# A two-layer graph network on one core: the stretch behind the softmax reordered by halves of the nodes

## The chip, the core and the metric

The kernel runs on one core of a Trainium2 chip. A core has TensorE (PE, matmuls; its weight loads have rows of their own, PEld), VectorE (DVE), ScalarE (ACT), GpSimd (POOL) and SyncE (SP, which only starts transfers here), and 16 DMA engines that all queues share. The metric is the device time of one execution in microseconds, lower is better.

## The reference

There are 256 nodes with 1024 features. Layer 0 sends messages over 8192 edges and ends in an update of the nodes, layer 1 is a graph attention without softmax. Both end in a residual sum and a layer norm over the features:

```python
# layer 0: alpha is a softmax per target over the edges' logits
z_f = segment_sum(alpha[:, None] * n_f[edge_src], edge_dst, N)
nf2 = concatenate([n_f, z_f], axis=1)                 # 256 x 2048
h_new = relu(nf2[:64] @ W_hn + b_hn)                  # nodes 0 to 63
o_new = relu(nf2[64:] @ W_on + b_on)                  # nodes 64 to 255
x1 = layernorm(x + concatenate([h_new, o_new]))
# layer 1
h = x1 @ W                                            # 256 x 1024
al, ar = h @ a_l, h @ a_r
e = exp(-leaky_relu(al[src] + ar[dst], 0.1))
h_prime = segment_sum(e[:, None] * h[dst], src, N) / (segment_sum(e, src, N)[:, None] + 1e-5)
out = layernorm(x1 + elu(h_prime))
```

## The kernel before

Half 0 is nodes 0 to 127 and half 1 is nodes 128 to 255; a tile holds one half on its 128 partitions. Every weight matrix is streamed in chunks of 128 rows x 1024 columns, two to a transfer, in the order of the list `stream`; chunk numbers n count along it. SP starts each transfer of two chunks into one of 4 places of `W_raw`, once the low parts of the two chunks that lay there are made. For each chunk ScalarE casts `W_raw` to fp32r (`W_hi`, line 432), and VectorE (`W_lo`, line 669) or GpSimd (line 364) subtracts that from the original; `by_pool(n)` gives every fourth chunk (n % 4 == 3) behind chunk 55 to GpSimd. The two parts stand in a ring of NB = 4 places, and a place is free once TensorE has counted the chunk four earlier as used (`chunk_used`). A product in full precision is then three products: high by high, high by low, low by high.

Each engine runs its own program in the order in which it is written, and the stages named in `PE_STAGES`, `ACT_STAGES` and `DVE_STAGES` are counts that the others wait for. `link` makes VectorE wait for its own last instruction.

**The update** (chunks 48 to 79, `update`, lines 1261 to 1283) takes `W_hn` and `W_on` alternately, two chunks of each. A chunk of `W_hn` costs 4 matmuls of 512 columns, which give nodes 0 to 63 (line 1273). A chunk of `W_on` costs 4 such for nodes 64 to 127 (line 1273) and 6 more for half 1 (line 1281). Each group of 4 puts the two parts of 64 nodes side by side on the 128 output partitions, so the two halves of partitions have to be added afterwards. The order within a chunk of `W_on` is half 0 first, half 1 behind it, chunk by chunk, up to chunk 79.

**Layer norm of layer 0** (lines 604 to 622 on ScalarE, 952 to 998 on VectorE): ScalarE copies the partitions to be added out of PSUM (stages q0_low, q1_low); VectorE adds the biases from `bn_bc`, the two parts, then relu and the residual; `bn_stats` and `bn_aggr` give mean and variance (line 957, 958), ScalarE the root (line 594), and the normalised half 0 is written by ScalarE (line 611), half 1 by VectorE (line 969). TensorE transposes each half (line 1317, stages x1T0, x1T1), ScalarE and VectorE make the high and low part of the transposed features.

**h** (chunks 80 to 87, `block_by_block`, line 1089): for each group of 4 chunks half 0, then half 1; 6 matmuls a chunk and half, 96 in all. The first matmul comes after both halves have been transposed. Behind the last, VectorE multiplies h by `a_l` and `a_r` with sums (line 1006), TensorE spreads the source scores over all partitions (line 1326), the exponentials times edge counts are made for all 256 x 256 pairs in `PT`, then TensorE makes the row sums (line 1331, 8 rows) and `h_prime` (line 1336, 16 rows: 4 products of 512 columns for each half, each in two rows).

**The end**: for each half ScalarE writes exp and relu of `h_prime` over the row sum (line 635), VectorE makes elu plus residual (lines 1032, 1034), the statistics and the second layer norm; SP starts one transfer of 512 KB for each half of the output (lines 316, 318). GpSimd subtracts one from `x1` for the elu (line 413) behind its last `W_lo`.

Of the kernel before, what the change touches and what calls it, by code (L numbers as in the profile page):

```python
# [16 lines left out]
Q = 64  # L17
# [22 lines left out]
def gnn_two_layers(nc, x, src, dst, W_hh, b_hh, W_oo, b_oo, W_ho, b_ho, W_a, b_a, W_hn, b_hn, W_on, b_on,  # L40
# [6 lines left out]
    with ctx:  # L47
# [36 lines left out]
        small = sb("small", [P, 64])  # L84

# [143 lines left out]
        for k in range(0, 2 * KC, 2):  # L229
            stream += [("hn", W_hn, k), ("on", W_on, k)]  # L230
# [3 lines left out]
        END = {"ooA": 8, "ooB": 16, "hoA": 30, "hh": 40, "hoB": 48, "updx": 64, "upd": 80, "h1": 88}  # L234
# [27 lines left out]
        def lo_count(n, pool):  # L262
# [27 lines left out]
        def _(sp):  # L290
# [24 lines left out]
            sp.wait_ge(act_step, act_at("out0"))  # L315
            sp.dma_start(out[0:P, :], y2[:, 0, :]).then_inc(out_in, 16)
            sp.wait_ge(dve_step, dve_at("out1"))
            sp.dma_start(out[P:N, :], y2[:, 1, :]).then_inc(out_in, 16)
            sp.wait_ge(out_in, 32)
# [3 lines left out]
        def _(pool):  # L323
# [86 lines left out]

            lows(END["hoB"] + NB, len(chunks))
# [5 lines left out]
        def _(act):  # L417
# [150 lines left out]
            act.dma_start(bn_bc[0:Q, 0, :], b_hn.partition_broadcast(Q)).then_inc(biases_in, 16)  # L568
            act.dma_start(bn_bc[Q:P, 0, :], b_on.partition_broadcast(Q)).then_inc(biases_in, 16)
            act.dma_start(bn_bc[:, 1, :], b_on.partition_broadcast(P)).then_inc(biases_in, 16)  # L570
# [5 lines left out]
            highs(END["hoB"], END["hoB"] + NB)  # L576
            act.wait_ge(dve_step, dve_at("maxima"))
# [13 lines left out]
            highs(UX + 4, END["upd"] - 2)  # L591
            def deviation(h):

                sa.activation(deviations[:, h:h + 1], small[:, 41 + 2 * h:42 + 2 * h], ACT.Sqrt, bias=eps_ln[:, 0:1]) \
                    .then_inc(act_step, 1)
# [11 lines left out]
            highs(END["upd"] - 2, END["upd"])  # L607

            def normalise_first_half(dest):

                sa.activation(dest, y1[:, 0, :], ACT.Identity, bias=small[:, 10:11], scale=small[:, 8:9]) \
                    .then_inc(act_step, 1)

            act.wait_ge(dve_step, dve_at("var0"))
            deviation(0)
            act.wait_ge(dve_step, dve_at("scale0"))
            normalise_first_half(x1[:, 0, :])
            act.wait_ge(dve_step, dve_at("var1"))
            deviation(1)
            for h in range(2):  # L620
                act.wait_ge(pe_step, pe_at(f"x1T{h}"))
                sa.copy(xT_hi[:, :, h * P:(h + 1) * P], G0[:, h * D:(h + 1) * D].rearrange("p (c n) -> p c n", n=P)) \
                    .then_inc(act_step, 1)
# [5 lines left out]
            act.wait_ge(dve_step, dve_at("lr"))  # L629
            sa.activation(PT[:], PT[:], ACT.Exp, scale=-1.0).then_inc(act_step, 1)  # L630
            act.wait_ge(dve_step, dve_at("row_sums"))
            for h in range(2):
                act.wait_ge(pe_step, pe_at(f"hp{h}"))
                for part, func in ((y2, ACT.Exp), (y1, ACT.Relu)):
                    sa.activation(part[:, h, :], G1[:, h * D:(h + 1) * D], func, scale=small[:, 6 + h:7 + h]) \
                        .then_inc(act_step, 1)
            warm_up(ACT.Sqrt, 0)
            act.wait_ge(dve_step, dve_at("var2"))
            deviation(0)
            act.wait_ge(dve_step, dve_at("scale2"))  # L640
            normalise_first_half(y2[:, 0, :])
            act.wait_ge(dve_step, dve_at("var3"))
            deviation(1)
# [3 lines left out]
        def _(dve):  # L647
# [289 lines left out]
            lows(UX, UX + NB)  # L937
            for s in range(2):
# [11 lines left out]
            lows(UX + NB + 4, END["upd"] + NB - 2)  # L950

            def statistics(h):

                for g in range(2):
                    link(v.bn_stats(small[:, 16 + 12 * h + 6 * g:22 + 12 * h + 6 * g], y1[:, h, g * 512:(g + 1) * 512]))  # L957
# [403 lines left out]
```

## Time and profile before

| | us |
|---|---|
| median of 3 runs | 383.04 |
| lowest and highest of them | 382.99 to 384.62 |
| profiled execution, its own time | 383.35 |
| its span, first to last instruction | 381.3 |
| TensorE busy, share of the span | 326.5, 86% |
| VectorE busy | 301.9, 79% |
| ScalarE busy | 189.9, 50% |
| GpSimd busy | 136.8, 36% |
| mean granted TensorE clock | 0.934 of 2.4 GHz |

The profiled execution's own time is its span plus 2.05 us. The span can be read in stages by the line numbers of the chain: up to 260 us the first part of layer 0, 260 to 311 us the update, 311 to 328 us the layer norm, 328 to 351 us h, and 351 us to the end scores, `h_prime` and output. Only what lies behind about 230 us is touched by the change.

### The profile page before, as it was taken

Reading aid. Unit: us, or ns where it says so; the run is one execution under the profiler, and the core shown is the slowest. Engines: PE = TensorE matmul, PEld = TensorE weight load, DVE = VectorE, ACT = ScalarE, POOL = GpSimd, SP = SyncE. Lnnn points to the kernel's source line nnn. Section 1 sums busy time; section 2 is a strip of 40 time slices with the busy share of each in tenths; the row PEclk is TensorE's granted clock in tenths of the full one; section 3 lists DMA queues with packets and bytes.
Section 4 is the critical chain, followed back from the end, with each engine's and each line's share of the span. In section 5 each row is a group of like instructions: output and inputs, shape, how many; then the busy total and the mean of one; then the engine's idle time right before and its main releaser. Section 6 shows DMA issues by size and latency. Waiting matters only on the chain.

```text
span 381.3 us, 4671 instructions
## 1 busy us (share of the span) xinstructions
PE 326.5 (86%) x1434; PEld 252.7 (66%) x1434; DVE 301.9 (79%) x400; ACT 189.9 (50%) x289; POOL 136.8 (36%) x202
## 2 busy tenths in 40 slices
PE   2899999999999998999999999638899962898570
PEld 1678877776547866888888887426688841686320
DVE  0799999959799687999999997985677789436445
ACT  3745594220333349788787764250566581251143
POOL 3200070370008002988988773910024231016000
PEclk9999999999999999999999999885999995699685
DMA  7997698899989960002003003333638960000002
GB/s 232 412 400 292 238 345 298 278 244 275 354 297 377 388 243 2 0 3 112 0 2 111 3 3 89 131 110 119 211 106 332 306 250 2 0 2 1 0 0 110
DMA packets 17639, 63.63 MB, mean 167 GB/s; under 512 B 2234, under 2 KB 2236, under 8 KB 17360
## 3 DMA queue, kind: packets, MB, share of 16 engines
q1 hardware_dynamic: 13520, 50.34, 36.2%
q0 software_dynamic: 2096, 8.74, 7.8%
q10 hardware_dynamic: 2000, 4.26, 3.2%
q8 instruction: 13, 0.21, 0.2%
q14 instruction: 10, 0.08, 0.1%
HBM read 60.16 MB, written 3.16 MB: 166 GB/s over the span
## 4 chain that ended last, share of the span: by engine, by line
PE 64%; DVE 25%; DMA 4%; ACT 4%; issue 2%; SPq 0%; DVEq 0%; ACTq 0%
PE ps L1240 20%; PE ps L1067 10%; PE ps L1131 7%; DVE W_lo L669 6%; PE ps L1089 6%; PE ps L1247 3%; PE ps L1273 3%; PE ps L1106 3%; PE ps L1304 3%; PE ps L1336 3%; DMA W_raw<-in_L_gnn_W_dram 2%; PE ps L1281 2%; DMA x_nat<-in_x_dram 2%; DVE tile_val L690 1%; DVE small L957 1%
## 5 line engine op out<-in xcount | busy, mean ns | idle before, releaser
L432 ACT CAST W_hi<-W_raw 128x1024 fp32r<-128x1024 f32 x72 | 73.2, 1046 | 67.9 <-DMA W_raw<-in_L_gnn_W_ho_dram 24.6
L669 DVE TENSOR_TENSOR W_lo<-W_raw,W_hi 128x1024 fp32r<-128x1024 f32 x56 | 73.7, 1342 | 23.2 <-ACT W_hi L432 20.7
L905 DVE SCALAR_TENSOR_TENSOR ps<-ps,wa_bc 128x1024 f32<-128x1024 f32 x74 | 87.6, 1277 | 1.9 <-PE ps L1240 1.9
L364 POOL TENSOR_TENSOR W_lo<-W_raw,W_hi 128x1024 fp32r<-128x1024 f32 x16 | 39.4, 2468 | 82.0 <-ACT W_hi L432 82.0
L1240 PE MATMUL ps<-A_tab,oh 128*128 x148 | 53.5, 443 | 2.2 <-ACT oh L541 2.2
L390 POOL TENSOR_SCALAR sc_r<-irow,keys 128x64 f32<-128x64 f32 x74 | 35.0, 472 | 39.1 <-PE ps L1247 38.7
L1067 PE MATMUL ps<-W_hi,xT_hi 128*128 128x512 f32 x112 | 46.5, 415 | 0.9 <-DVE W_lo L669 0.9
L1240 PE MATMUL ps<-B_tab,oh 128*128 x148 | 46.4, 394 | 0.0
L1067 PE MATMUL ps<-W_lo,xT_hi 128*128 128x512 f32 x112 | 44.1, 394 | 0.0
L547 ACT ACTIVATE sc_l<-sc_l,keys 128x64 f32<-128x64 f32 x74 | 24.6, 341 | 21.8 <-DVE ps L905 15.5
L1067 PE MATMUL ps<-W_hi,xT_lo 128*128 128x512 f32 x112 | 34.5, 390 | 0.0
L391 POOL TENSOR_SCALAR sc_l<-irow,keys 128x64 f32<-128x64 f32 x74 | 33.0, 446 | 0.0
L1247 PEld LDWEIGHTS ps<-sc_r,sc_l 128*128 128x128 f32 x148 | 27.4, 189 | 6.3
L1240 PEld LDWEIGHTS ps<-B_tab,oh 128*128 128x128 f32 x148 | 27.8, 188 | 4.9
L1131 PE MATMUL ps<-W_raw,hh_x 128*128 128x512 f32 x64 | 28.2, 594 | 0.0
L1240 PEld LDWEIGHTS ps<-A_tab,oh 128*128 128x128 f32 x148 | 24.1, 187 | 4.0 <-issue 3.5
L1067 PEld LDWEIGHTS ps<-W_hi,xT_hi 128*128 128x128 f32 x112 | 21.3, 190 | 7.3 <-DVE W_lo L669 2.5
L534 ACT ACTIVATE oh_dist<-key_rows,pcol 128x512 bf16<-128x512 uint8 x37 | 26.1, 707 | 0.0
L1067 PEld LDWEIGHTS ps<-W_lo,xT_hi 128*128 128x128 f32 x112 | 21.4, 191 | 4.7 <-issue 0.7
L1067 PEld LDWEIGHTS ps<-W_hi,xT_lo 128*128 128x128 f32 x112 | 21.2, 189 | 4.6
L1247 PE MATMUL ps<-sc_r,sc_l 128*128 128x64 f32 x148 | 24.0, 247 | 0.0
L541 ACT ACTIVATE oh<-oh_dist 128x512 fp32r<-128x512 bf16 x37 | 23.1, 625 | 0.9 <-PE ps L1240 0.6
(229 smaller groups left out, 546.7 us busy)
## 6 DMA issues: line engine op xcount, KB each, us to landing
W_raw<-in_L_gnn_W_oo_dram SPq DMA_DIRECT2D x8, 1024.0 KB, 9.7
W_raw<-in_L_gnn_W_ho_dram SPq DMA_DIRECT2D x8, 1024.0 KB, 4.9
W_raw<-in_L_gnn_W_hh_dram SPq DMA_DIRECT2D x8, 1024.0 KB, 8.4
W_raw<-in_L_gnn_W_hn_dram SPq DMA_DIRECT2D x8, 1024.0 KB, 5.3
W_raw<-in_L_gnn_W_on_dram SPq DMA_DIRECT2D x8, 1024.0 KB, 6.0
W_raw<-in_L_gnn_W_dram SPq DMA_DIRECT2D x4, 1024.0 KB, 7.6
key_rows<-key_rows_scratch POOLq DMA_DIRECT2D x1, 2304.0 KB, 14.0
table_scratch<-tabs ACTq DMA_DIRECT2D x2, 1024.0 KB, 6.4
```

The costliest lines, as they stand in the source:

```text
L364: ga.tensor_tensor(W_lo[:, ring(n), :], W_raw[:, n // 2 % NS, n % 2, :], W_hi[:, ring(n), :].bitcast(F32), ALU.subtract).then_inc(lo_pool, 1)
L390: ga.tensor_scalar(sc_r[:, t % U, :], irow[:, 1:Q + 1], keys[:, t, 0:1], None, ALU.is_equal)
L391: ga.tensor_scalar(sc_l[:, t % U, 1, :], irow[:, 1:Q + 1], keys[:, t, 1:2], None, ALU.is_equal) \
L432: sa.copy(W_hi[:, ring(n), :], W_raw[:, n // 2 % NS, n % 2, :]).then_inc(hi_made, 1)
L534: sa.activation(oh_dist[:, j % 2, :, :], key_rows[:, :, 2 * j * P:2 * (j + 1) * P], ACT.Abs, bias=pcol[:, 1:2]).then_inc(dist_made, 1)
L547: sa.activation(sc_l[:, t % U, 0, :], sc_l[:, t % U, 1, :], ACT.Copy, scale=keys[:, t, 2:3]) \
L669: v.tensor_tensor(W_lo[:, ring(n), :], W_raw[:, n // 2 % NS, n % 2, :], W_hi[:, ring(n), :].bitcast(F32), ALU.subtract).then_inc(lo_made, 1)
L905: v.scalar_tensor_tensor(acc, acc, 0.0, wa_bc[:], ALU.max, ALU.mult, accum_out=keys[:, t, 2:3]).then_inc(reduced, 1)
L1067: ins = mm(acc[:, m * D + f:m * D + f + 512], x_part(n - first, m), W[:, f:f + 512], start=(n == first and x_part is hi and W is W1), stop ...
L1131: ins = mm(G0[:, f:f + 512], hh_x[:, row // KC, row % KC, :], W_raw[:, n // 2 % NS, n % 2, f:f + 512], start=(row == 0), stop=(row == 2 * ...
L1240: ins = mm(acc[:, n * 512:(n + 1) * 512], oh[:, t // 2 % 2, k, t % 2 * P:(t % 2 + 1) * P], tab[:].rearrange("p q d -> p (q d)")[:, n * 512 ...
L1247: ins = mm(G0[:, bass.ds(column.with_bounds(min_val=0, max_val=15 * Q), Q)], sc_l[:, t % U, :, :].rearrange("p r n -> p (r n)"), sc_r[:, t ...
```

## The change

1. **Order of the update.** The stream takes `W_hn` ahead of `W_on`, so that chunks 76 to 79 are the last four of `W_on` and `W_hn` is through at chunk 75. For chunks 76 to 79 the matmuls of half 0 (`parts` 0) are issued for all four chunks, and the 24 of half 1 behind them. `chunk_used` counts these chunks with the matmuls of half 1. ScalarE then copies q0_low, q1_low between its casts.
2. **Biases by matmul.** The two bias rows come to 64 partitions only, are split into a high and a low part on ScalarE (stage parts) and VectorE, and six matmuls of 512 columns with a pattern `pick` of ones (made by GpSimd) add them into PSUM at the beginning of the update. The additions from `bn_bc` go.
3. **Layer norms.** The sums come with the instruction that adds the residual (`accum_out`); `bn_stats` goes. ScalarE squares the half less its mean, with a sum (`Square`, `deviation`), then takes the root (`root`). Both halves are normalised by VectorE. Residual and partitions of half 0 are merged in two instructions for each 64 nodes (`merge`).
4. **Half 0 leads.** TensorE transposes half 0, starts the first two chunks of h for half 0, and only then transposes half 1. The low parts of chunks 83 and 87 move from GpSimd to VectorE; GpSimd subtracts one from `x1` right behind the transposes.
5. **h and scores.** The last four chunks are multiplied for half 0 (stage h_0), then columns 0 to 511 of half 1 (h_1), then columns 512 to 1023. The scores of half 1 are made in two parts of 512 columns and added. `PT` goes through leaky relu, exp and edge counts by halves.
6. **h_prime and the end.** `h_prime` of half 0 comes ahead of the row sums, half 1 behind them in two parts of 512 columns. Relu is taken before the division and scaled by VectorE. The root's table of ScalarE is no longer called up ahead of the second layer norm. The second output half is normalised half by VectorE and half by ScalarE, and its two parts are started by SP and by ScalarE's queue.

```diff
+        update_order = [("hn", 0), ("on", 0), ("hn", 2), ("on", 2), ("hn", 4), ("on", 4), ("hn", 6), ("hn", 8), ("on", 6),
+                        ("hn", 10), ("on", 8), ("hn", 12), ("on", 10), ("hn", 14), ("on", 12), ("on", 14)]
...
-            return n % 4 == 3
+            return n % 4 == 3 and n < END["upd"]
...
+            pool.wait_ge(gathered, NT)
+            link(ga.memset(pick_f[:], 0.0))
+            for r in (0, Q // 2):
+                link(ga.memset(pick_f[r:r + 1, 0:P], 1.0))
+            ga.nop().then_inc(pick_made, 1)
             lows(END["hoB"] + NB, len(chunks))
...
+            act.wait_ge(pick_made, 1)
+            sa.copy(pick[:], pick_f[:])
+            act.wait_ge(biases_in, 112)
+            sa.copy(bn_parts[:], bn_rows).then_inc(act_step, 1)
             act.wait_ge(dve_step, dve_at("maxima"))
...
+            def deviation(h, waste):
+                sa.activation(waste, y1[:, h, :], ACT.Square, bias=less_mean[:, h:h + 1], accum_out=squares[:, h:h + 1]) \
+                    .then_inc(squared, 1)
+            def root(h, nth):
+                act.wait_ge(squared, nth)
+                sa.activation(deviations[:, h:h + 1], squares[:, h:h + 1], ACT.Sqrt, bias=eps_ln[:, 0:1], scale=1.0 / D) \
...
+            highs(END["hn"], END["hn"] + 2)
+            act.wait_ge(dve_step, dve_at("mean0"))
+            deviation(0, x1[:, 0, :])
+            root(0, 1)
+            highs(END["hn"] + 2, END["upd"])
+            x1_high(0)
+            act.wait_ge(dve_step, dve_at("mean1"))
+            deviation(1, x1[:, 1, :])
+            root(1, 2)
+            x1_high(1)
...
+            link(v.tensor_tensor(bn_parts[Q // 2:Q], bn_rows[Q // 2:Q], bn_parts[Q // 2:Q].bitcast(F32), ALU.subtract))
+            stage("parts")
...
+            dve.wait_ge(act_step, act_at("q0_low"))
+            merge(G0[0:Q, D:2 * D], y2[0:Q, 0, :], slice(0, Q))
+            dve.wait_ge(act_step, act_at("q1_low"))
+            merge(G1[Q:P, 0:D], y2[Q:P, 0, :], slice(Q, P))
+            mean(0, "mean0")
+            low(END["upd"])
+            inverse(0, "sd0")
+            normalise(x1[:, 0, :], y1[:, 0, :], 0)
+            stage("x1_0")
+            dve.wait_ge(chunk_used, END["upd"])
+            link(v.scalar_tensor_tensor(y1[:, 1, :], G1[:, D:2 * D], 0.0, x_nat[:, 1, :], ALU.max, ALU.add,
+                                        accum_out=y_sums[:, 1:2]))
+            mean(1, "mean1")
+            low(END["upd"] + 1)
+            x1_low(0)
+            inverse(1, "sd1")
+            normalise(x1[:, 1, :], y1[:, 1, :], 1)
...
+            for h in range(2):
+                dve.wait_ge(act_step, act_at(f"exp{h}"))
+                link(v.tensor_tensor(PT[:, h, :], PT[:, h, :], S_cnt[:, 0, h, :], ALU.mult))
+                stage(f"ET{h}")
...
+            update(70, END["hn"])
+            update(END["hn"], END["upd"], (0,))
+            update(END["hn"], END["upd"], (1,))
...
+            transpose_x1(0)
+            pe.wait_ge(dve_step, dve_at("x1T0"))
+            for n in range(END["upd"], END["upd"] + NB):
+                h_chunk(n, 0, (0, 512))
+                if n == END["upd"] + 1:
+                    transpose_x1(1)
+            pe.wait_ge(dve_step, dve_at("x1T1"))
+            for n in range(END["upd"], END["upd"] + NB):
+                h_chunk(n, 1, (0, 512)).then_inc(chunk_used, 1)
...
+            act.wait_ge(dve_step, dve_at("scale3"))
+            sa.activation(y2[:, 1, 512:D], y1[:, 1, 512:D], ACT.Identity, bias=small[:, 10:11], scale=rstd[:, 1:2]) \
+                .then_inc(act_step, 1)
+            act.wait_ge(act_step, act_at("out3"))
+            act.dma_start(out[P:N, 512:D], y2[:, 1, 512:D]).then_inc(out_in, 16)
```

## Rows read from the trace of the kernel before

**Rows 1.** Chain that ended last, from 290 us: start us, us, what.

```profile
327.90 23.49 PE ps L1089 x96
...
359.64 9.76 PE ps L1336 x16
```

**Rows 2.** Timeline of TensorE: start us, us, line, operation, tiles, count, idle before.

```profile
308.43 0.39 PE L1273 MATMUL ps<-W_hi,z_both 128*128 128x512 f32 x1
...
310.30 0.62 PE L1281 MATMUL ps<-W_hi,zT_lo 128*128 128x512 f32 x2
322.16 1.97 PE L1317 MATMUL ps<-ident,x 128*128 128x128 f32 x8 [11.24 <-ACT x L611]
...
331.25 0.40 PE L1089 MATMUL ps<-W_hi,xT_hi 128*128 128x512 f32 x1
...
350.75 0.61 PE L1089 MATMUL ps<-W_hi,xT_lo 128*128 128x512 f32 x2
...
357.78 1.86 PE L1331 MATMUL ps<-ones_f,PT 128*128 128x1 f32 x8 [4.00 <-DVEq L663]
```

**Rows 3.** Timeline of VectorE, 310 to 356 us.

```profile
310.24 1.22 DVE L976 TENSOR_TENSOR y<-y,bn_bc 64x1024 f32<-64x1024 f32 x1
...
317.29 1.42 DVE L957 BATCH_NORM_STATS2 small<-y 128x6 f32<-128x512 f32 x2
...
320.36 0.16 DVE L963 RECIPROCAL small<-deviations 128x1 f32<-128x1 f32 x1
...
324.47 0.81 DVE L969 TENSOR_SCALAR x<-y,small 128x1024 f32<-128x1024 f32 x1
...
326.57 1.22 DVE L994 TENSOR_TENSOR xT_lo<-ps,xT_hi 128x1024 fp32r<-128x1024 f32 x1
...
347.31 2.23 DVE L1009 TENSOR_SCALAR y<-ident,small 128x128 f32<-128x128 f32 x1
...
355.53 0.69 DVE L1018 SCALAR_TENSOR_TENSOR PT<-PT 128x512 f32<-128x512 f32 x1
```

**Rows 4.** Timeline of ScalarE, 303 to 368 us.

```profile
303.05 1.05 ACT L432 CAST W_hi<-W_raw 128x1024 fp32r<-128x1024 f32 x1 [2.19 <-DMA W_raw<-in_L_gnn_W_on_dram]
...
307.61 1.28 ACT L599 ACT_TABLE_LOAD   x1
...
309.12 1.01 ACT L604 COPY y<-ps 64x1024 f32<-64x1024 f32 x1
...
320.87 1.24 ACT L611 ACTIVATE x<-y,small 128x1024 f32<-128x1024 f32 x1 [1.52 <-DVEq L663]
...
356.31 0.63 ACT L630 ACTIVATE PT<-PT 128x512 f32<-128x512 f32 x1 [0.87 <-DVEq L663]
...
366.44 2.12 ACT L635 ACTIVATE y<-ps,small 128x1024 f32<-128x1024 f32 x2 [9.50 <-DVEq L663]
```

**Rows 5.** Timeline of GpSimd.

```profile
305.59 2.42 POOL L364 TENSOR_TENSOR W_lo<-W_raw,W_hi 128x1024 fp32r<-128x1024 f32 x1 [4.16 <-ACT W_hi L432]
...
344.08 5.39 POOL L413 TENSOR_SCALAR x<-x 128x2048 f32<-128x2048 f32 x1
```

**Rows 6.** Windows of 1 us: PE, PEld, DVE, ACT, POOL busy, PEclk, DMA share, GB/s.

```profile
313.00:314.00 1.00, 0.00 (x0) 0.00 (x0) 0.96 (x2) 0.18 (x1) 0.74 (x1) 0.95 0.04 16
...
330.00:331.00 1.00, 1.00 (x3) 0.76 (x3) 0.00 (x0) 0.00 (x0) 0.00 (x0) 0.52 0.00 0
...
354.00:355.00 1.00, 0.00 (x0) 0.00 (x0) 0.82 (x3) 0.57 (x1) 0.00 (x0) 0.93 0.00 0
...
365.00:366.00 1.00, 1.00 (x3) 0.48 (x3) 0.01 (x1) 0.00 (x0) 0.00 (x0) 0.95 0.00 0
```

**Rows 7.** Timeline of SP's queue: the last transfer of the output.

```profile
378.26 0.36 SPq L318 DMA_DIRECT2D out_dram<-y  x1
```

**Rows 8.** Timelines of ScalarE and VectorE, 249 to 269 us.

```profile
249.94 1.76 ACT L579 ACTIVATE S_log<-S_log,small 128x768 f32<-128x768 f32 x2 [8.93 <-DVEq L663]
...
267.86 1.23 DVE L941 TENSOR_TENSOR zT_lo<-ps,zT_hi 128x1024 fp32r<-128x1024 f32 x1 [4.21 <-ACT zT_hi L584]
```

More of the change, by code:

```diff
@@ L84, in gnn_two_layers @@
         small = sb("small", [P, 64])
+        dots, dot_parts = (small[:, k:k + 4].rearrange("p (h k) -> p h k", h=2) for k in (34, 38))
+        y_sums, less_mean, squares, rstd = (small[:, k:k + 4] for k in (46, 50, 54, 58))
         eps_ln = sb("eps_ln", [P, 1])
@@ new lines, in mean, with inverse, normalise, x1_low @@
+            def mean(h, name):
+                link(v.tensor_scalar(less_mean[:, h:h + 1], y_sums[:, h:h + 1], -1.0 / D, None, ALU.mult))
+                stage(name)
+            def inverse(h, deviation):
+                dve.wait_ge(act_step, act_at(deviation))
+                link(v.reciprocal(rstd[:, h:h + 1], deviations[:, h:h + 1]))
+            def normalise(dest, part, h):
+                link(v.tensor_scalar(dest, part, less_mean[:, h:h + 1], rstd[:, h:h + 1], ALU.add, ALU.mult))
+            def x1_low(h):
@@ new lines, in source_dots @@
+            def source_dots(h):
+                link(v.tensor_scalar(y2[:, 0, h * P:(h + 1) * P], ident[:], dots[:, h, 0:1], None, ALU.mult))
+            dve.wait_ge(biases_in, 80)
+            dve.wait_ge(pe_step, pe_at("h_0"))
+            for k in range(2):
+                dot(0, k, 0, D, dots[:, 0, k:k + 1])
+            stage("dots0")
+            source_dots(0)
+            dve.wait_ge(pe_step, pe_at("h_1"))
+            for k in range(2):
+                dot(1, k, 0, 512, dot_parts[:, 0, k:k + 1])
@@ L1258, in _, with update @@
                     scatter(t - LAG, column)
-            def update(a, b):
+            def update(a, b, parts=(0, 1)):
                 for n in range(a, b):
@@ L1319, in _, with h_chunk @@
                 stage(ins, f"x1T{h}")
-            for g in range(END["upd"], END["h1"], NB):
-                block_by_block(g, G1, END["upd"], "x1T", "h_0" if g + NB == END["h1"] else None)
+            def h_chunk(n, m, columns):
+                W1, W0 = split_chunk(n)
+                c = n - END["upd"]
+                for part, Ws in ((xT_hi, (W1, W0)), (xT_lo, (W1,))):
+                    for f in columns:
+                        for W in Ws:
+                            ins = mm(G1[:, m * D + f:m * D + f + 512], part[:, c, m * P:(m + 1) * P], W[:, f:f + 512],
+                                     start=(c == 0 and part is xT_hi and W is W1), stop=(c == KC - 1 and part is xT_lo))
+                return ins
@@ L1341 @@
+            stage(ins, "sums")
+            for n in range(2):
+                for hd in range(2):
+                    ins = hp(1, n, hd)
+                stage(ins, f"hp{1 + n}")
 _INS = ['x', 'src', 'dst', 'L0_gnn_W_hh', 'L0_gnn_b_hh', 'L0_gnn_W_oo', 'L0_gnn_b_oo', 'L0_gnn_W_ho', 'L0_gnn_b_ho',
```

281 lines of the change are left out of this document (128 added, 153 removed).

## The prediction

> **What bounds the kernel now.** I read first the windows, then the chain of waits, then the timelines of the engines behind 300 us. TensorE leads up to the end of the update: its matmuls follow each other at (310.30 - 308.43) / 8 = 0.234 us, and the last ends at 310.92 [rows 2]. From there it waits 11.24 us for the layer norm, and the reader should see who works: VectorE, one linked instruction behind the other (biases, parts, residual, statistics), with ScalarE's root and normalising between. The first matmul of h comes at 327.90, and 96 of them take 23.49 us, to 351.39 [rows 1]. The scores are again VectorE with ScalarE between, until TensorE starts the row sums at 357.78 [rows 2]; `h_prime` ends at 369.40 [rows 1]. The rest, 11.9 us, is exp and relu, elu, statistics, root, normalising and the last transfer, started at 378.26 [rows 7]. So five legs, measured on the axis of before:
>
> - end of update to h: 310.92 to 327.90, 17.0
> - h: 23.5
> - end of h to the first product with `PT`: 6.4
> - sums and `h_prime`: 11.6
> - `h_prime` to the end of the span: 11.9
>
> In four of the five TensorE idles or runs at half clock. The windows show the clock: it stood at 2.4 GHz through the update, fell to 1.2 late in the window from 313 (3 us into idleness) and rose at the end of the window from 330, some 3.1 us into h; it fell again in the window from 354 and rose in that from 365, over 7 us after the sums had begun [rows 6].
>
> **The update, part by part.** The six bias matmuls lie on TensorE, which leads here: 6 x 0.234 = 1.4 us of loss. Their preparation does not: ScalarE's two casts (192 and 2048 columns, by the 1.01 us of a 64x1024 copy [rows 4] about 2.2) fit into its idle 8.93 us, VectorE's subtraction of 2048 columns (twice 1.22, so 2.4) into its idle 4.21 [rows 8]. Without that cover the softmax chain would be later by up to 4.6. GpSimd's three memsets fall where it waits for the next cast. Transfers shrink from three bias pieces to two.
>
> The order of the chunks alone costs nothing: 24 chunks of either kind stay, and I walked the ring through chunk by chunk. It gets tight once. Part 0 of chunks 76 to 79 needs all four in the ring within 12 x 0.234 = 2.8 us of the end of chunk 75, but chunk 79 can be cast only when 75 is used: 0.25 + 1.05 for the cast [rows 4], 2.42 for its low part, which is GpSimd's [rows 5], together 3.8. TensorE stalls about 1.0. The cast of chunk 78 waited for its transfer until 303.05 [rows 4], so up to 0.9 more is possible; no stall at all is the other bound. I take 1.0. Update ends at 310.9 + 1.4 + 1.0 = 313.3, but part 0 is through 24 x 0.234 = 5.6 earlier, at 307.7.
>
> **Update to h.** ScalarE: cast of 79 ends 304.1, table load and warm-up 1.5 (1.28 the load [rows 4]), q0_low 305.6 to 306.6, q1_low 307.9 to 308.9. Behind it stand the casts of 80 and 81, which wait for part 1 of chunks 76 and 77 and end at 311.7: a new place in the queue, ahead of the squares. VectorE: four instructions of the 1.22 kind [rows 3], with an accumulated sum some 0.05 more, from 306.7 to 311.9, mean to 312.1. That is late enough for the casts to hide by 0.4 us. Squares 1.24 [rows 4] plus 0.2 for the reading of the sum, which no row shows (bounds 0 and 0.4), root 0.3, reciprocal 0.16 [rows 3], normalise 0.81 [rows 3], 0.1 for each hand-over: x1_0 at 315.2. Before, transposes began at 322.16 [rows 2].
>
> Transposes at half clock 1.97 [rows 2], high part 1.0, low part 1.22 [rows 3]: h starts at about 319.7 where it was 327.90. Between these VectorE takes the residual of half 1 (1.25), its mean and the low part of 81 (1.23), done before the high part arrives. Leg: 319.7 - 310.9 = 8.8, plainly 8.2 less.
>
> The Trainium skill speaks against one edit here: "ScalarE: Activation LUTs", rules for kernel authors, would have multiplying done on VectorE. For this dtype the rows don't bear out a penalty (1.24 for 1024 columns on ScalarE against 1.22 on VectorE), and by the rule the sum would have a VectorE pass of about that length in its place, the same time. The same page has a switch of table set at about 2.7 us, load and drain; our load row has 1.28 with the warm-up right behind it, so the measurement decides.
>
> **h.** Matmuls at full clock are (350.75 - 331.25) / 86 = 0.227 apart [rows 2], so 96 take 21.8, and before, the slow start cost 1.7. Now 8 transposes of half 1 lie inside (half of 1.97, so 1.0). They hide the second transposing, high and low part behind chunks 80 to 83 of half 0. The low parts of 82 and 83 are ready at 323.6, before they are needed; for 84 to 87 VectorE follows the casts and each is ready over 1 us ahead. The clock: TensorE now idles 1.9 us, transposes, idles 2.4, which I take as enough for the fall. How long it stays at 1.2 GHz has bounds in the rows, 3.1 us (h) and 7.3 us (sums and `h_prime`); I take 4.7, which costs half, 2.35. No fall would give that back and 1.0 of the transposes. Leg 21.8 + 1.0 + 2.35 = 25.1, to 344.8: 1.6 more than before.
>
> **End of h to `PT`.** h_0 comes 24 matmuls (5.4) before the end, so the two products of half 0 and half a product of half 1 are done by then. Left: a half product (0.69 [rows 3]), two tiny ones at 0.2, the diagonal 0.3, the spreading matmul under the second half product, then for half 0: add 0.5, leaky relu 0.4, and exp of half 1's scores runs under it. An exp of 512 columns took 0.63 and a multiply 0.69 [rows 3, 4]; for 256 I take 0.4 each. `PT` of half 0 is ready at 349.5, 4.7 after h: 1.7 less. The diagonal that took 2.23 beside GpSimd's 5.39 us [rows 3, 5] lay before the end of h and gives nothing by itself; GpSimd's work now lies at 325 to 330, beside a low part that reads PSUM.
>
> **Sums and `h_prime`.** 3 of 8 products at half clock (1.7 each), 5 at full (0.86), the sums in the middle at full clock, half of their 1.86 [rows 2]: 5.1 + 4.3 + 0.95 = 10.4, to 359.9. 1.2 less. The bounds: no fall, 2.6 less; all at half, 4.3 more.
>
> **The end.** Half 0 of `h_prime` is through 4.4 us earlier than half 1; the sums come at 356.5, exp of half 0 ends at 358.0 (two instructions took 2.12 [rows 4], relu is already done). From here VectorE leads: elu and sum of half 0 2.5, mean 0.2, of half 1 in two parts 2.9, sum and mean 0.4: 364.1. Before, 1.42 + 0.21 of statistics [rows 3] lay in this for each half. Squares with the sum 1.45, root 0.4, reciprocal and shift 0.45, normalise half a tile on ScalarE 0.85, and the ScalarE queue's start at 367.5. The table load (1.28) lies between square and root of half 0, whose root comes at 364.0, when VectorE is about to ask: hidden by 0.1. From the last start to the end of the span were 3.04 us; half the size and a longer issue give 2.7. End at 370.2: leg 10.3, 1.6 less.
>
> **Sum.** -8.2 + 1.6 - 1.7 - 1.2 - 1.6 = -11.1. From the profiled execution's 383.35 that is 372.25; the median lies 0.3 below it, so I forecast 372.0, 2.9% faster.
>
> **The rivals.**
> - *Square has no place in the root's or the exp's table.* The load rows show three switches only, and copies, relu and identity ran without one, for and against nothing about Square. Each pair square and root would then load twice (2.56): one pair on the path ahead of h, one behind `h_prime`. 372.0 + 5.1 = 377. [...] 7%.
> - *The front gains less.* Supply of chunks 77 to 79 late by a transfer, and ScalarE's casts of 80 and 81 then delay the squares one for one: 2 of stall more and 1.5 in the queue. 375.5. For it: the transfer wait at 303.05; against: transfers are now asked for slightly earlier than before. 10%.
> - *The clock turns the sign.* The gaps in the new order of h (transposes inside, waits for low parts) keep TensorE at 1.2 GHz throughout: 96 x 0.227 again instead of 2.35, 19.4 more, 391. It becomes no gain when the slow stretch has grown by 22 us, that is all of h. Against it: in the update TensorE had the same chunk-wise waits and full clock. 2%.
> - *The gain goes nowhere*, because the clock falls in h and in `h_prime` for the longest (1.3 + 4.3) and other small costs of new instructions and hand-overs (some 40, at 0.1) add 4: 381.5. 4%, about half of it within 0.5%.
>
> **How the numbers follow.** Forecast 77%, with its own range 368.5 (no fall of the clock in h, 3.4) to 375.5 (clock 1.3, stall 0.9, unseen readings 1.2). Rivals 7, 10, 2, 4%. The range 368.5 to 376.0 holds the forecast and the second rival, less the forecast's tails, about 8 in 10. A measurement of this kernel tells 0.5% from no change. Faster 0.95, same 0.02, slower 0.03.
>
> **What would show it.** Update: six matmuls behind chunk 59, a gap near 1 us before the last four of part 0, the end 2.4 us later, relative to the start of the update. Layer norm: no `BATCH_NORM` rows, first transpose 2 us behind the last update matmul instead of 11.2. h: first matmul 8 us earlier, clock back within 5 us. Before `PT`: 4.7 us. End: VectorE without idle from exp of half 0 to the mean of half 1, one table load between square and root. I am wrong if two loads surround a square, if VectorE idles for ScalarE's squares because casts stand ahead, or if the first `h_prime` products are slow for longer than 5 us.

## The result and the profile after

| | before | after |
|---|---|---|
| median | 383.31 us (4 runs) | 372.11 us (4 runs) |
| lowest to highest | 382.99 to 384.62 | 371.43 to 373.84 |
| profiled execution, its own time | 383.35 | 373.84 |
| its span | 381.3 | 371.7 |
| mean granted TensorE clock | 0.934 | 0.951 |

The ratio is 0.971 with an interval from 0.9673 to 0.9747; 372.0 was forecast. What follows are the lines of the changed kernel that answer to those shown of before. Here its timeline of TensorE:

```profile
279.20 1.65 PE L1363 MATMUL ps<-bn_parts,pick 64*128 64x512 f32 x6
...
308.37 0.50 PE L1322 MATMUL ps<-W_hi,z_both 128*128 128x512 f32 x1 [1.03 <-POOL W_lo L372]
...
316.23 1.10 PE L1374 MATMUL ps<-ident,x 128*128 128x128 f32 x8 [1.05 <-DVEq L701]
320.30 0.79 PE L1384 MATMUL ps<-W_hi,xT_hi 128*128 128x512 f32 x1 [2.98 <-DVEq L701]
...
325.38 1.03 PE L1374 MATMUL ps<-ident,x 128*128 128x128 f32 x8
...
346.95 0.70 PE L1406 MATMUL ps<-y,ones_f 128*128 128x256 f32 x2 [1.44 <-DVEq L701]
350.74 6.22 PE L1410 MATMUL ps<-h,PT 128*128 128x512 f32 x8 [3.10 <-DVEq L701]
```

The wait of 11.24 us ahead of the transposes [rows 2] is 1.05 now: the update ends at 315.18 and the layer norm of half 0 lies beside its last 24 matmuls. The second transposes stand inside h. ScalarE, from the casts of chunks 77 to 79 to the first square, and at the end:

```profile
302.65 2.95 ACT L445 CAST W_hi<-W_raw 128x1024 fp32r<-128x1024 f32 x3 [1.29 <-PE ps L1330]
305.62 1.28 ACT L622 ACT_TABLE_LOAD   x1
...
307.12 1.01 ACT L632 COPY y<-ps 64x1024 f32<-64x1024 f32 x1
...
309.60 1.01 ACT L634 COPY y<-ps 64x1024 f32<-64x1024 f32 x1 [1.46 <-PE ps L1322]
...
313.50 1.15 ACT L611 ACTIVATE x<-y,small 128x1024 f32<-128x1024 f32 x1
314.56 0.18 ACT L611 ACTIVATION_READ_ACCUMULATOR x<-y,small 128x1 f32 x1
...
363.43 0.20 ACT L611 ACTIVATION_READ_ACCUMULATOR h<-y,small 128x1 f32 x1
363.65 1.28 ACT L617 ACT_TABLE_LOAD   x1
364.94 0.29 ACT L617 ACTIVATE deviations<-small,eps_ln 128x1 f32<-128x1 f32 x1
```

No table load stands ahead of a square: one load ahead of the first layer norm, one between square and root of the second. VectorE, from the first merge to the normalised half, and the scores:

```profile
308.17 1.22 DVE L997 TENSOR_TENSOR ps<-ps,y 64x1024 f32<-64x1024 f32 x1 [2.08 <-ACT y L632]
309.43 1.22 DVE L998 SCALAR_TENSOR_TENSOR y<-ps,x_nat 64x1024 f32<-64x1024 f32 x1
...
315.31 0.81 DVE L1013 TENSOR_SCALAR x<-y,small 128x1024 f32<-128x1024 f32 x1
...
349.12 0.48 DVE L1073 TENSOR_SCALAR PT<-ps,small 128x256 f32<-128x256 f32 x1
349.64 0.42 DVE L1074 SCALAR_TENSOR_TENSOR PT<-PT 128x256 f32<-128x256 f32 x1
350.21 0.99 DVE L1078 TENSOR_TENSOR PT<-PT,S_cnt 128x256 f32<-128x256 f32 x2
```

And the clock, in windows of 1 us (columns as in [rows 6]; PEclk stands behind the busy share of POOL):

```profile
318.00:319.00 1.00, 0.00 (x0) 0.00 (x0) 1.00 (x2) 1.00 (x2) 0.00 (x0) 0.65 0.00 0
...
325.00:326.00 1.00, 1.00 (x8) 0.82 (x8) 0.00 (x0) 0.00 (x0) 0.00 (x0) 0.93 0.00 0
...
349.00:350.00 1.00, 0.00 (x0) 0.00 (x0) 0.84 (x2) 0.42 (x1) 0.00 (x0) 0.51 0.00 0
...
355.00:356.00 1.00, 1.00 (x3) 0.39 (x2) 0.00 (x0) 0.00 (x0) 0.00 (x0) 0.57 0.00 0
```

It fell to 1.2 GHz in the window from 318, behind the first transposes, which therefore took 1.10 us and not 1.97 [rows 2]. It was back at about 325, 4.8 us into h. It fell again in the window from 349 and was back late in that from 355, 5 us into the products with `PT`.

**Legs.** Executions of one kernel differ by 0.6 to 4.4 us, and the profiled executions differ in places that no edit touches (the last section), so the legs of the profiled executions, one for each kernel, are the finer measure. Point A is the start of the second update matmul behind the last product that aggregates messages (273.68 before, 274.72 after). From A, in us:

| kernel | time, us | ratio, interval | A to end of update | A to h | h | end of h to `PT` product | sums, `h_prime` | end | A to end |
|---|---|---|---|---|---|---|---|---|---|
| before | 383.3 to 383.6 | 1 | 37.24 | 54.22 | 23.46 | 6.42 | 11.60 | 11.92 | 107.62 |
| after | 372.11 | 0.971, 0.9673 to 0.9747 | 40.46 | 45.58 | 25.21 | 5.23 | 10.55 | 10.41 | 96.98 |
| e1 | 375.79 | 0.9784, 0.9749 to 0.9819 | 39.01 | 48.66 | 25.44 | 5.23 | 10.68 | 10.43 | 100.44 |
| e2 | 374.16 | 0.9741, 0.9720 to 0.9763 | 40.46 | 48.37 | 24.01 | 5.24 | 10.82 | 10.49 | 98.93 |
| e3 | 369.63 | 0.9653, 0.9629 to 0.9677 | 40.40 | 45.52 | 23.00 | 5.23 | 10.92 | 10.48 | 95.15 |
| e4 | 370.01 | 0.9650, 0.9629 to 0.9670 | 40.43 | 45.55 | 25.15 | 5.24 | 8.02 | 10.49 | 94.45 |
| e5 | 372.84 | 0.9722, 0.9695 to 0.9749 | 39.34 | 45.52 | 24.59 | 5.24 | 10.12 | 10.41 | 95.88 |
| e6 | 368.97 | 0.9612, 0.9588 to 0.9637 | 39.32 | 45.51 | 23.00 | 5.25 | 8.03 | 10.45 | 92.24 |
| e7 | 374.79 | 0.9771, 0.9748 to 0.9794 | 40.44 | 45.55 | 25.21 | 5.81 | 10.23 | 11.06 | 97.86 |
| e8 | 376.24 | 0.9813, 0.9788 to 0.9839 | 40.40 | 45.53 | 24.53 | 5.24 | 10.42 | 13.32 | 99.04 |
| e9 | 366.35 | 0.9547, 0.9523 to 0.9571 | 39.38 | 44.51 | 23.03 | 4.54 | 8.37 | 10.41 | 90.86 |
| e10 | 372.52 | 0.9696, 0.9662 to 0.9730 | 40.45 | 45.55 | 25.27 | 5.23 | 10.60 | 10.48 | 97.13 |
| e11 | 371.94 | 0.9691, 0.9664 to 0.9718 | 40.00 | 45.11 | 24.56 | 5.22 | 10.62 | 10.45 | 95.96 |
| e12 | 371.97 | 0.9696, 0.9668 to 0.9725 | 40.43 | 45.54 | 24.58 | 4.53 | 10.64 | 10.47 | 95.76 |

The reader should see how still most columns stand (A to h is 45.52 to 45.58 wherever nothing ahead of h was changed), and which two do not: h, 24.5 or 25.2 for the same instructions, and sums with `h_prime`, 10.1 to 10.9.

### The profile page after: what moved, and what is told of

The parts are those of the page before. It is cut to its first block, busy times and chain, and to the rows that moved or that the text cites. A ratio compares the mean times of both kernels' runs of the same rounds, so it can differ in the third digit from the quotient of the medians.

```text
span 371.7 us, 4709 instructions
## 1 busy us (share of the span) xinstructions
PE 327.9 (88%) x1440; PEld 252.5 (68%) x1440; DVE 293.2 (79%) x411; ACT 195.8 (53%) x300; POOL 134.6 (36%) x203
## 3 DMA queue, kind: packets, MB, share of 16 engines
q1 hardware_dynamic: 13520, 50.07, 36.9%
## 4 chain that ended last, share of the span: by engine, by line
PE 69%; DVE 21%; ACT 4%; issue 2%; DMA 2%; POOL 1%; SPq 0%; DVEq 0%; ACTq 0%
PE ps L1288 21%; PE ps L1135 10%; PE ps L1179 7%; PE ps L1384 7%; PE ps L1322 5%; DVE W_lo L707 4%; PE ps L1330 4%; PE ps L1295 3%; PE ps L1154 3%; PE ps L1354 3%; DMA x_nat<-in_x_dram 2%; PE ps L1410 2%; ACT W_hi L445 1%; DVE tile_val L728 1%; PE ps L1211 1%
## 5 line engine op out<-in xcount | busy, mean ns | idle before, releaser
L445 ACT CAST W_hi<-W_raw 128x1024 fp32r<-128x1024 f32 x72 | 73.2, 1046 | 63.1 <-DMA W_raw<-in_L_gnn_W_ho_dram 24.6
L707 DVE TENSOR_TENSOR W_lo<-W_raw,W_hi 128x1024 fp32r<-128x1024 f32 x58 | 70.7, 1243 | 21.2 <-ACT W_hi L445 18.2
L372 POOL TENSOR_TENSOR W_lo<-W_raw,W_hi 128x1024 fp32r<-128x1024 f32 x14 | 35.4, 2538 | 48.3 <-ACT W_hi L445 48.3
L560 ACT ACTIVATE sc_l<-sc_l,keys 128x64 f32<-128x64 f32 x74 | 24.5, 341 | 20.9 <-DVE ps L943 14.5
```

The lines of the kernel that those rows point to most:

```text
L372: ga.tensor_tensor(W_lo[:, ring(n), :], W_raw[:, n // 2 % NS, n % 2, :], W_hi[:, ring(n), :].bitcast(F32), ALU.subtract).then_inc(lo_pool, 1)
L445: sa.copy(W_hi[:, ring(n), :], W_raw[:, n // 2 % NS, n % 2, :]).then_inc(hi_made, 1)
L707: v.tensor_tensor(W_lo[:, ring(n), :], W_raw[:, n // 2 % NS, n % 2, :], W_hi[:, ring(n), :].bitcast(F32), ALU.subtract).then_inc(lo_made, 1)
```

## The experiments

Each kernel is the changed one with the edit named. Legs are those of the table above; "time" is the median.

**e1: the last four chunks of the update not split** (half 0 and half 1 of each chunk together again).

```diff
-            update(END["hn"], END["upd"], (0,))
-            update(END["hn"], END["upd"], (1,))
+            update(END["hn"], END["upd"])
```

> The changed kernel with one edit: chunks 76 to 79 are multiplied whole, half 0 and half 1 of each chunk, not half 0 of all four ahead. My theory (the layer norm of half 0 is a serial leg that begins when half 0 of the update ends): the stall on chunk 79 of 1.2 us goes, but the last matmul of half 0 comes 1.4 us before the end of the update in place of 5.6, so VectorE's merge of nodes 64 to 127 starts about 3.2 us later, and TensorE idles over 5 us, so that the first transposes run at half clock (1.0 more). Time 4 us longer than the changed kernel, about 376. Rival (the gain lies in the instructions that were taken out, not in who leads): no change beyond 0.5 us, or 1 us faster, by the stall.

A to h grew by 3.1 (48.66), the time by 3.7. The timeline of TensorE: there is no stall, and relative to A the update ends 1.45 sooner, but the transposes wait again and meet the slow clock.

```profile
312.34 0.63 PE L1330 MATMUL ps<-W_hi,zT_lo 128*128 128x512 f32 x2
318.24 1.97 PE L1373 MATMUL ps<-ident,x 128*128 128x128 f32 x8 [5.26 <-DVEq L701]
```

So the split is worth 3.1 of the 8.6 us that A to h lost against before. The other 5.5 are left to the layer norm's shorter chain and to half 0 going first. e2 undoes the second of these; no run undoes the first, so its share is a remainder and not measured.

**e2: half 1 transposed ahead of h** (`transpose_x1(1)` right behind `transpose_x1(0)` and not inside h).

```diff
             transpose_x1(0)
+            transpose_x1(1)
             pe.wait_ge(dve_step, dve_at("x1T0"))
...
-                if n == END["upd"] + 1:
-                    transpose_x1(1)
```

> The changed kernel with one edit: both halves are transposed before the first matmul of h, as before the change; layer norm untouched. Theory: x1 of half 1 is ready at 321.4 us, the transposes end about 323.4, so h starts 3 us later, and 1.0 us of transposes leaves h: 2 us longer, about 374. If the transposes inside h had cost more than they hid, this would be no slower.

A to h grew by 2.8. h shrank by 1.2: the 8 transposes (1.03) have left it, and its stretch at 1.2 GHz was 4.2 and not 4.8 (from 321.74 until the clock was back at 325.9). Both legs together are 1.6 longer, the time 2.1. Timeline of TensorE:

```profile
320.12 1.97 PE L1374 MATMUL ps<-ident,x 128*128 128x128 f32 x8 [4.13 <-DVEq L701]
```

**e3 and e4: matmuls whose result is thrown away, to keep the clock.** e3 puts 12 of them behind the first transposes, e4 puts 5 and 12 around the spreading of the source scores. They write to a part of PSUM that is overwritten later.

```diff
+            def fill(count, acc):
+                for _ in range(count):
+                    mm(acc, zT_hi[:, 0, 0:P], zT_hi[:, 0:2, :].rearrange("p c n -> p (c n)"), start=True, stop=True,
+                       skip_group_check=True)
...
             transpose_x1(0)
+            fill(12, G1[:, 0:512])
             pe.wait_ge(dve_step, dve_at("x1T0"))
```

is e3, and with the same function

```diff
+            fill(5, G0[:, D:D + 512])
             pe.wait_ge(dve_step, dve_at("al"))
             stage(mm(G0[:, 0:N], ones_f[:], y2[:, 0, 0:N], start=True, stop=True), "albc")
+            fill(12, G0[:, D:D + 512])
```

is e4.

> The changed kernel with 12 more matmuls of 512 columns, whose result is thrown away, between the transposes of half 0 and h, where TensorE idles 3 us. Theory (half the slow start of h is the clock): the clock stays at 2.4 GHz, the first 11 matmuls of h come 0.2 us closer to each other each, h is 2.3 us shorter and the time 2.3 us shorter, about 369.8. Rival (h is paced by the low parts of chunks 80 to 83): the clock rises and a wait takes the place of the slow matmuls, under 0.5 us gained.

> The changed kernel with 5 thrown-away matmuls behind h and 12 behind the spreading of the scores, where TensorE idles 1.4 and 3.1 us. Theory: the three products of h_prime at half clock go from 1.7 to 0.86 us, 2.5 us less, and since exp of half 0 waits for them, the whole time is 2.5 shorter, about 369.6. Rival: the fillers delay the spreading matmul or the first product, up to 0.5 us lost, and VectorE's chain hides what TensorE gains.

e3: h 23.00, 2.2 less; sums and `h_prime`, which the edit doesn't touch, took 0.4 more in this execution, the other legs moved by less than 0.1, and from A it is 1.8 less. The time is 2.5 less. e4: sums and `h_prime` 8.02, 2.5 less, and no other leg moved by 0.1; the time is 2.1 less. A window of e3 at the place where the clock had fallen, and the timeline of e4:

```profile
319.00:320.00 1.00, 1.00 (x6) 0.84 (x5) 1.00 (x1) 0.00 (x0) 0.00 (x0) 1.00 0.00 0
```

```profile
346.04 3.10 PE L1373 MATMUL ps<-zT_hi 128*128 128x512 f32 x12
349.49 3.70 PE L1417 MATMUL ps<-h,PT 128*128 128x512 f32 x8 [0.34 <-DVEq L701]
```

Eight rows that took 6.22 take 3.70. The price of the slow clock is thus measured at both places, 1.6 to 2.2 (h, against 24.6 and 25.2) and 2.5.

**e5: the low part of chunk 79 made by VectorE**, to take away the stall of 1.03.

```diff
-            return n % 4 == 3 and n < END["upd"]
+            return n % 4 == 3 and n < END["upd"] - 1
```

> The changed kernel with the low part of chunk 79 made by VectorE in place of GpSimd. Theory (TensorE's stall in part 0 is GpSimd's 2.6 us for that one low part): VectorE has it about 1.3 us after the cast, the stall of 1.2 us goes nearly whole, and as q1_low waits for part 0 and VectorE for q1_low, all that follows is 1.1 us earlier: about 371.0. Rival (the stall is the cast or the transfer, and only the engine named changes): no gain.

This theory fell. The stall is gone and the update ends 1.12 sooner (39.34), but A to h stands at 45.52 where it was 45.58. The transposes now wait for that time (timeline of TensorE, ScalarE and VectorE):

```profile
313.46 1.44 PE L1374 MATMUL ps<-ident,x 128*128 128x128 f32 x8 [2.10 <-DVEq L701]
```

```profile
299.90 2.95 ACT L445 CAST W_hi<-W_raw 128x1024 fp32r<-128x1024 f32 x3 [1.29 <-PE ps L1330]
302.87 1.28 ACT L622 ACT_TABLE_LOAD   x1
304.17 0.20 ACT L622 ACTIVATE warm<-eps_ln 128x1 f32<-128x1 f32 x1
304.38 1.01 ACT L632 COPY y<-ps 64x1024 f32<-64x1024 f32 x1
305.77 1.01 ACT L634 COPY y<-ps 64x1024 f32<-64x1024 f32 x1 [0.38 <-PE ps L1322]
```

```profile
305.43 1.22 DVE L997 TENSOR_TENSOR ps<-ps,y 64x1024 f32<-64x1024 f32 x1 [0.94 <-ACT y L632]
```

Against the start of the last three casts, the first merge begins at 5.53 here and at 5.52 in the changed kernel. It waits for the copy of quarter 0, and that stands on ScalarE behind the cast of chunk 79 and 1.5 us of table load. The stall on TensorE and the table load on ScalarE lie beside each other, and either alone keeps the layer norm where it is. The chain of the changed kernel's profile had gone through the stall; it was one of two ways of equal length, as e9 and e10 below show: its second merge begins at 310.71, right behind both its first merge (310.65) and the copy of quarter 1 (310.61).

**e6: e3, e4 and e5 in one kernel.**

> The changed kernel with all three: thrown-away matmuls ahead of h and around the spreading of the scores, and the low part of chunk 79 on VectorE. If the three legs are serial, as my sum has them, the gains add: 2.3 + 2.5 + 1.1 = 5.9 less, about 366.2. If one hides another (a clock that is kept in h also being kept later, or the other way round), less than 5 in all.

The two fills add up (h 23.00, sums and `h_prime` 8.03) and chunk 79 adds nothing (45.51). From A 4.7 less, not 5.9: what is missing is the 1.1 forecast for chunk 79, and neither fill hides the other. The profiled executions differ by 4.6 (369.24 against 373.84, which was the changed kernel's longest), the medians by 3.1 only.

**e7: the row sums ahead of `h_prime`**, as before the change.

```diff
-            stage(ins, "hp0")
...
             stage(ins, "sums")
+            for hd in range(2):
+                for n in range(2):
+                    ins = hp(0, n, hd)
+            stage(ins, "hp0")
```

> The changed kernel with the row sums ahead of h_prime of half 0, both behind PT of both halves, as before the change. Theory (VectorE's last chain begins with exp of half 0, and that with the sums): TensorE starts 0.5 us later and the sums run at half clock (1.9 in place of 0.95), relu then still stands ahead of exp on ScalarE; exp of half 0 ends 1.0 to 1.8 us later and so does everything: about 373.5. Rival (TensorE's total alone counts): 1.4 us or, where the chain has slack, under 0.5.

From A 0.9 more, a little under the 1.0 of the theory; the time 2.7 more (all of its runs within 374.29 to 374.93, those of the changed kernel 371.43 to 373.84), of which the legs explain only the 0.9. The legs show where: the first matmul with `PT` waits for both heads (5.81, 0.6 more), and the end is 0.7 longer (11.06), since relu of half 0 now stands on ScalarE ahead of exp. The eight tiny sums run at half clock, but sums and `h_prime` together take 0.3 less (10.23), so that costs nothing here. Timeline of TensorE:

```profile
351.21 1.87 PE L1417 MATMUL ps<-ones_f,PT 128*128 128x1 f32 x8 [3.67 <-DVEq L701]
```

**e8: `bn_stats` again in the second layer norm** in place of squares on ScalarE.

```diff
-            deviation(0, h1[:, 0, :])
-            root(0, 3)
...
+            def statistics(h, name):
+                for g in range(2):
+                    link(v.bn_stats(small[:, 16 + 12 * h + 6 * g:22 + 12 * h + 6 * g], y1[:, h, g * 512:(g + 1) * 512]))
+                link(v.bn_aggr(small[:, 12 + 2 * h:14 + 2 * h], small[:, 16 + 12 * h:28 + 12 * h]))
...
-            mean(0, "mean2")
+            statistics(0, "mean2")
```

> The changed kernel with mean and variance of the second layer norm by bn_stats and bn_aggr on VectorE again, the root alone on ScalarE. Theory (VectorE leads the end): its chain grows by 1.6 us for each half less the 0.15 to 0.4 of the means, 2.7 in all, and ScalarE's pass of 1.35 us with its sum leaves the way ahead of the last root: 1.3 to 1.5 us longer, about 373.5. Rival (squares on ScalarE are as long on the path as the statistics were on VectorE): no change beyond 0.3.

The end grew by 2.9, twice what I had expected; from A it is 2.1 more (h came at 24.53 in this execution), the time 4.1 more. VectorE's timeline:

```profile
360.34 1.42 DVE L1095 BATCH_NORM_STATS2 small<-y 128x6 f32<-128x512 f32 x2
361.80 0.21 DVE L1096 BATCH_NORM_AGGREGATE small<-small 128x2 f32<-128x12 f32 x1
...
365.39 1.42 DVE L1095 BATCH_NORM_STATS2 small<-y 128x6 f32<-128x512 f32 x2
...
367.59 0.81 DVE L1011 TENSOR_SCALAR y<-y,small 128x1024 f32<-128x1024 f32 x1
368.55 0.16 DVE L1007 RECIPROCAL small<-deviations 128x1 f32<-128x1 f32 x1
```

Both statistics lie on the path, 1.6 and 1.5 more than a mean by sums. The squares of half 1 that go had cost 1.35, but the normalising of half 0 had lain beside them, and that (0.96 with its hand-over) now stands ahead of the reciprocal of half 1, so only 0.4 comes back. That cover is what I had left out. With the statistics the end is also 1.4 longer than before the change (13.32 against 11.92). So the other edits of the end, half 1 in two parts and the normalising of half 0 moved to VectorE among them, don't pay by themselves; which of them costs this, no run tells.

**e10, e9: the table load between the two copies.** e10 is the changed kernel with this edit alone. e9 has it with e6, and the first head finished ahead of the second (e12, below), with 10 instead of 12 thrown-away matmuls.

```diff
-            warm_up(ACT.Sqrt, 0)
-
             act.wait_ge(chunk_used, END["hn"])
             sa.copy(y2[0:Q, 0, :], G0[Q:P, D:2 * D]).then_inc(act_step, 1)
+            warm_up(ACT.Sqrt, 0)
```

> The changed kernel with the table load of Sqrt between ScalarE's two copies, and nothing else. Theory (stall and table load cover each other): with the stall of chunk 79 still there, the copy of quarter 0 and its merge come 1.5 us sooner, but the copy of quarter 1 still waits for its product (309.60 in the changed kernel), so the mean and h move by the little that VectorE's two merges of quarter 0 reach beyond that copy, 0.1 us at most: 372.0 us. Rival (the table load alone is what holds the merges): 1.0 to 1.3 us less, 371.0.

> The changed kernel with the throw-away matmuls ahead of h and in the scores (10 instead of 12 behind the second score product), the second parts of chunk 79's weights made on VectorE, the table load of Sqrt moved from ahead of ScalarE's first copy of quarter 0 to between its two copies, and the first head's scores finished (exp, times count) before the second head's are begun. Theory (e5 gained nothing because the merges begin with the copy of quarter 0, which stands on ScalarE behind the cast of chunk 79 and the 1.28 + 0.20 us of the table load): against the run with fills and chunk 79 on VectorE, the first merge begins 1.5 us sooner against that cast, and of this 1.1 to 1.2 us reach h, since the copy of quarter 1 then waits for its own product; the first head's product begins 0.6 us sooner: span less the time up to the first copy of the scores 1.7 us shorter, 128.2, and about 367.3 us in time. Rival (the merges are held by the update's own end on TensorE, not by ScalarE's queue): first transposes at the same distance from the cast as before, 129.4 and 368.4 us.

e10: 45.55, nothing, as e5 alone gave nothing. e9: 44.51, 1.0 less than e6 and 1.07 less than the changed kernel. That settles e5's question: with both stall and table load A to h is 45.58, with the table load alone 45.52 (e5), with the stall alone 45.55 (e10), with neither 44.51 (e9). (The fills, which e9 also has, don't move this leg: 45.51 in e6.) VectorE's timeline of e9 shows the merge following its own low part without idle time:

```profile
303.74 3.50 DVE L706 TENSOR_TENSOR W_lo<-W_raw,W_hi 128x1024 fp32r<-128x1024 f32 x3 [0.84 <-ACT W_hi L445]
307.15 1.21 DVE L996 TENSOR_TENSOR ps<-ps,y 64x1024 f32<-64x1024 f32 x1
```

e9 takes 366.35 us, 4.5% less than before, and is the fastest kernel of the study.

**e12: the first head's scores finished ahead of the second's.**

```diff
                 stage(f"lr{h}")
-            for h in range(2):
                 dve.wait_ge(act_step, act_at(f"exp{h}"))
                 link(v.tensor_tensor(PT[:, h, :], PT[:, h, :], S_cnt[:, 0, h, :], ALU.mult))
```

> The changed kernel with the first head's exp and product with the counts ahead of the second head's sums on VectorE. Theory: the first head's product on TensorE starts 0.6 us sooner, and the second head's operand, 0.9 us later than now, is hidden behind its two matmuls at the lower clock (3.1 us): 0.6 us less, 371.5 us. Rival (the second head's operand becomes the wait, or the copy of h on ScalarE does, which now ends at about the time of lr1): no gain, within 0.2 us of 372.1.

End of h to the first product fell from 5.23 to 4.53, and sums and `h_prime` stayed (10.64). The time, 371.97, cannot tell 0.7 us from nothing. In e9, at full clock, 0.35 of it is lost again (8.37 against 8.03), since the second head's operand is then late for its matmuls: it is ready at 348.77, while the first head's two matmuls, 0.86 each, end at about 348.5. The first eight rows, 3.70 in e4, take 4.04. Timelines of TensorE and VectorE in e9:

```profile
346.82 4.04 PE L1416 MATMUL ps<-h,PT 128*128 128x512 f32 x8
```

```profile
348.34 0.43 DVE L1076 TENSOR_TENSOR PT<-PT,S_cnt 128x256 f32<-128x256 f32 x1 [0.54 <-ACT PT L651]
```

**e11: the six bias matmuls left out** (the result lacks `b_hn` and `b_on`).

> The changed kernel without the six matmuls that add the biases b_hn and b_on to the sums (these two biases are left out of the result). Theory: they stand on TensorE's path with all of their 1.65 us, so that the update ends 1.65 us sooner and the time is 370.5 us. Rival (the casts, which wait for TensorE to give slots back, or VectorE's and GpSimd's second parts hold the update anyway): 0.5 us or less, 371.7 us.

My theory fell: of their 1.65 us A to h gives back 0.47. The timeline of TensorE shows what most of the rest turned into:

```profile
280.81 0.39 PE L1322 MATMUL ps<-W_lo,z_both 128*128 128x512 f32 x1
282.11 0.50 PE L1322 MATMUL ps<-W_hi,z_both 128*128 128x512 f32 x1 [0.91 <-POOL W_lo L372]
```

Chunk 63's low part comes from GpSimd (2.44 us), and in the new order chunks 60 to 63 are all of `W_hn`, 4 matmuls each, so TensorE reaches chunk 63 too early. The bias matmuls stand just ahead of that place and fill the wait.

## Why the prediction was right, step by step

In the profiled executions the span up to A is 1.04 longer than before, all of it ahead of the first copy of the scores (235.25 before, 236.37 after), from a dip of the clock in unchanged code (last section). From A it is 10.64 shorter; the forecast was 11.1 shorter, and the medians differ by 11.2. That the median was met to 0.1 is luck: the leg up to h gave 0.4 more than forecast, the wait for `PT` 0.5 less, and medians move by more than 0.1 from one set of runs to the next (383.3 to 383.6 for the kernel before). By the prediction's own terms:

- **Preparation of the biases hidden**: right. The stretch from VectorE's first copy of the scores of layer 0 to A took 38.43 before and 38.35 after, with the clock low for the same time in both.
- **Update 2.4 later**: 3.22. The six matmuls took 1.65, not 6 x 0.234; the stall was 1.03 (1.0 forecast); some 0.4 more comes with the split (e9, without a stall, 39.38 against 39.01 in e1). But neither of the two prices is what it costs the kernel: without the stall h starts no sooner (e5), and without the bias matmuls 0.47 sooner (e11). "The order of the chunks alone costs nothing" is wrong by about the same amount: without the bias matmuls TensorE waits 0.91 at chunk 63. My walk through the ring had not shown it.
- **h starts 8.2 sooner**: 8.64 (54.22 to 45.58). The normalised half 0 was forecast for 315.2 and came, less the 1.04, at 315.1. The transposes met the full clock, 0.9 less than I had put down; half of that went again, since VectorE made the low part of 81 until 319.0 and was 0.5 late for the low part of the transposed features, where I had it done in time. The start of ScalarE's squares behind two casts was forecast as hidden by 0.4, and it ties (cast until 313.5, mean at 313.4). The comparison of 1.24 on ScalarE with 1.22 on VectorE holds for instructions with two tensor operands, as a square by multiplying would be; normalising 1024 columns takes VectorE 0.81 [rows 3] against ScalarE's 1.24 [rows 4].
- **h 25.1**: 25.21, with a slow stretch of 4.8 where I had taken 4.7. That the 4.7, picked inside a range of 3.1 to 7.3, came so close was luck: in the profiles of e8, e11 and e12 the same code gives 24.5 to 24.6.
- **End of h to `PT` 4.7**: 5.23. This term was sized wrong. I let the exp of the second head run under the first, but VectorE's program has the second head's add and leaky relu (349.12 to 350.06) ahead of the product with the counts. e12 reorders them and measures 0.70 less, 4.53.
- **Sums and `h_prime` 10.4**: 10.55. **End 10.3**: 10.41, with the table load hidden as forecast.

Of the rivals, the square's tables and the supply of the last chunks are ruled out by the rows of after; the slow clock throughout h did not come; no gain was lost on the way.

The Trainium skill, "ScalarE: Activation LUTs" (What ACT_TABLE_LOAD costs), sets a switch at 1.28 us of load and 1.38 of drain. The load is 1.28 here; the root's instruction begins 1.29 behind the load's start, and nothing like a drain of that length stands on either side (0.02 ahead of it), so here the measurement decides for the smaller sum. "TensorE: Matmul & The Clock Gate" (What's actually happening) says of the slow start that "it's run-variable". The traces agree, with h at 24.5 or 25.2 for the same instructions.

## What to carry to other kernels

- A stall that the chain of waits names is worth its length only if no second way of the same length lies beside it. Ask what the next instruction on each engine would wait for with the stall gone; here stall and table load cost 1.07 us together, and taking away one alone gained less than 0.1.
- Work put on the leading engine is not a cost where that engine would soon have waited, and an order that "costs nothing" may owe it to such work. Walk the ring once without the new work too.
- TensorE's waits cost twice, as time and as slow clock behind them: 12 and 17 thrown-away matmuls in the waits ahead of h and ahead of `h_prime` gave 4 to 4.7 us by the legs, and by the medians 3.1 (e6 against the changed kernel) to 3.9 (e6 against e5).

## What was not expected of the hardware

The same code meets the clock differently in different executions, in at least three places: the first copy of the scores stands between 235.16 and 237.56 in the 14 profiled executions, A 36.9 to 38.5 behind it, and h takes 24.5 to 25.3 where nothing in it or just ahead of it was changed. At the aggregation behind the softmax the changed kernel's clock came back at about 267, and in e12, which is level with it up to there within 0.1 us, before 265. Windows of 1 us, the changed kernel:

```profile
264.00:265.00 1.00, 1.00 (x4) 0.82 (x3) 0.97 (x2) 0.00 (x0) 0.00 (x0) 0.50 0.46 66
...
267.00:268.00 1.00, 1.00 (x6) 0.88 (x5) 0.04 (x1) 0.15 (x1) 0.00 (x0) 0.95 0.88 361
```

and e12:

```profile
264.00:265.00 1.00, 1.00 (x4) 0.81 (x3) 0.97 (x2) 0.00 (x0) 0.00 (x0) 0.58 0.51 49
```

A comes 1.1 us sooner in e12. The beginning of the gather is another such place: in the profile of the kernel before the clock stays full there, in that of the changed kernel it dips for about 3 us (windows from 144 to 147). This dip sorts the 14 profiled executions: the first copy of the scores comes at 235.16 to 235.43 in the five without it (before, e1, e3, e4, e5), at 236.25 to 236.68 in the eight with it, and at 237.56 in e6, where it lasts twice as long.

```profile
144.00:145.00 1.00, 0.52 (x1) 0.50 (x2) 0.00 (x0) 0.97 (x3) 0.00 (x0) 0.61 0.00 0
...
147.00:148.00 1.00, 1.00 (x4) 0.78 (x4) 0.90 (x2) 0.00 (x0) 0.00 (x0) 0.68 0.07 16
```

This is why the single execution of e5 that was profiled (369.97) said nothing about its edit: with five more its median was 372.84. An edit worth under 1 us, as e12's, was to be seen only in a leg of the trace.
